# A four-layer residual kernel on one core: x1 goes through memory and back, the step's order changes, and the scores wait by halves

## Chip, cores and metric

The kernel runs on 1 core of one Trainium2 chip. The metric is the device time of one execution in microseconds (us), median of several runs.

## What is computed

`x` is 64 sequences of 64 tokens of 512 float32 numbers. Four layers follow each other, each added to its input:

```python
x0 = x  + x @ W.T + ((x @ A[a].T) @ Bm[a].T) * s[a]      # layer 0: dense, plus an adapter of rank 16 chosen per sequence
x1 = x0 + einsum('bct,bcd->bdt', x0, w1[b])              # layer 1: a 64 x 64 matrix chosen per sequence mixes the tokens
x2 = x1 + attention(x1; Wq, Wk, Wv, Wo, beta)            # layer 2: 16 heads of 32, causal, softmax over 64 tokens
y  = x2 + einsum('bct,bcd->bdt', x2, w3[c])              # layer 3: as layer 1
```

## The kernel before

The 4096 rows of `x` are worked off in 16 pairs of tiles of 128 rows (four sequences a pair). Everything is float32. The dense products are split in two float32r parts (`..._hi`, `..._lo`) and made of three products, hi by hi, hi by lo, lo by hi. The identity of layers 0, 1 and 3 is added to their matrices.

The order on each engine is written out by hand, with semaphores between the engines. After a prologue that turns and splits the five weight matrices and does layers 0 and 1 and the projections of pair 0, there are 16 steps. `in_steps` writes out step 0, loops over steps 1 to 12, and writes out 13 to 15. Step i on TensorE (`step`, L659) is:

1. `values(i)` (L566): the V projection of pair i, 24 matmuls of 512 columns;
2. `layer2_out(i-1)` (L632), 24 matmuls: the output projection of the pair before;
3. `layer0_dense(i+1)`, `adapters_up(i+1)` (L505, L511), 24 and 2 matmuls, into the banks `MIX`;
4. `turn_probs` (L596): transposes of the softmax's rows of pair i, eight for each half g, and between them `layer3(i-1)` and `layer1(i+1)` (both `mix`, L524);
5. `turn_x1(i+1)` (L535): eight transposes of `x1`, since the projections need it with its 512 columns on the partitions (`x1T`); two of VectorE's and ScalarE's copies of PSUM then make `x1T_hi` and `x1T_lo`;
6. `attend()` (L608), probabilities by V for pair i;
7. `key_part` and `query_part` (L556, L561), four of each, for pair i+1: 96 matmuls of 256 columns;
8. `adapters_down(i+2)` (L483), the small product of x with the chosen adapters, and `scores(i+1)` (L581), 64 products of 32 x 64.

The softmax of pair i runs beside 1 to 3. VectorE adds the mask and takes the row maxima (L1029, L1034), GpSimd subtracts them (L1211), ScalarE takes the exponential (L856), VectorE sums and inverts (L1038, L1040). Half 0 is scaled on GpSimd, half 1 on VectorE (L1043). `x` itself is loaded in an arrangement of blocks (`x_blocks`), so that one VectorE transpose of 32 x 32 blocks (`turn_x`, L969) gives `xT` with no TensorE work. GpSimd keeps a copy of `x1` for the residual (`keep_x1`, L1219), which `add_x1` (L1055) adds to layer 2's product. SyncE issues the loads and stores in program order (L395): adapters' rows (`gather_b`, 12 transfers a pair), the store of y, the four block loads of x, and the gathers of w3 and w1.

A matmul of unsplit float32 counts twice in the trace (a `x4` in the program is a `x8` there).

## Time and profile before

| | |
|---|---|
| median of 3 runs (lowest to highest) | 645.58 us (644.78 to 645.97) |
| the profiled execution, its own time | 645.96 us |
| its span from first to last instruction | 644.2 us |
| TensorE busy | 624.6 us, 97% |
| VectorE, ScalarE, GpSimd busy | 389.2 (60%), 211.7 (33%), 140.9 us (22%) |
| granted TensorE clock | full in every one of 40 slices |
| bytes moved | 31.48 MB, mean 49 GB/s |

Busy time says where an engine has work, not what ends last. So this case is read step by step: the time between the same instruction in two steps is what a step costs, and the start of each stage within it tells what each piece holds TensorE for. The duration of a single matmul is longer than its share, since matmuls overlap. The distance from one start to the next is what counts.

### The profile page before, as it was taken

Reading aid. Unit: us, or ns where it says so; the run is one execution under the profiler, and the core shown is the slowest. Engines: PE = TensorE matmul, PEld = TensorE weight load, DVE = VectorE, ACT = ScalarE, POOL = GpSimd, SP = SyncE. Lnnn points to the kernel's source line nnn. Section 1 sums busy time; section 2 is a strip of 40 time slices with the busy share of each in tenths; the row PEclk is TensorE's granted clock in tenths of the full one; section 3 lists DMA queues with packets and bytes.
Section 4 is the critical chain, followed back from the end, with each engine's and each line's share of the span. In section 5 each row is a group of like instructions: output and inputs, shape, how many; then the busy total and the mean of one; then the engine's idle time right before and its main releaser. Section 6 shows DMA issues by size and latency. Waiting matters only on the chain.

```text
span 644.2 us, 19674 instructions
## 1 busy us (share of the span) xinstructions
PE 624.6 (97%) x7814; PEld 524.6 (81%) x7814; DVE 389.2 (60%) x546; ACT 211.7 (33%) x404; POOL 140.9 (22%) x118
## 2 busy tenths in 40 slices
PE   5999999999999999999999999999999999999998
PEld 5787977879888787988879797887988878798885
DVE  3557675656567565666656557565656755556464
ACT  4534333332233232233322223332223323222322
POOL 2005041220403113040310404022040311304031
PEclk9999999999999999999999999999999999999999
DMA  8530102102030110203011020210203011010101
GB/s 266 161 102 20 48 6 61 40 20 73 4 90 8 57 41 13 81 4 90 8 52 46 5 87 5 65 33 22 72 3 90 8 57 42 16 49 2 39 1 66
DMA packets 41110, 31.48 MB, mean 49 GB/s; under 512 B 15546, under 2 KB 30906, under 8 KB 41082
## 3 DMA queue, kind: packets, MB, share of 16 engines
q1 hardware_dynamic: 37130, 25.06, 13.4%
q10 hardware_dynamic: 3952, 6.03, 2.8%
q8 instruction: 19, 0.31, 0.2%
q14 instruction: 9, 0.07, 0.0%
HBM read 22.15 MB, written 8.91 MB: 48 GB/s over the span
## 4 chain that ended last, share of the span: by engine, by line
PE 91%; DVE 4%; DMA 1%; issue 1%; ACT 1%; POOL 0%; ACTq 0%; DVEq 0%
PE banks L547 10%; PE banks L552 9%; PE banks L548 9%; PE banks L599 5%; PE banks L524 5%; PE banks L573 5%; PE banks L641 5%; PE banks L648 5%; PE banks L642 5%; PE banks L575 4%; PE banks L500 4%; PE banks L577 4%; PE banks L498 4%; PE banks L502 4%; PE banks L591 4%; PE banks L615 3%
## 5 line engine op out<-in xcount | busy, mean ns | idle before, releaser
L1211 POOL TENSOR_TENSOR probs<-probs,row_max 128x1024 f32<-128x1024 f32 x32 | 60.9, 1905 | 320.9 <-DVE row_max L1034 320.9
L547 PE MATMUL banks<-x1T_hi,w_hi 128*128 128x256 f32 x512 | 130.6, 287 | 0.2 <-DVE beta L1172 0.2
L548 PE MATMUL banks<-x1T_hi,w_lo 128*128 128x256 f32 x512 | 128.2, 283 | 0.0
L547 PEld LDWEIGHTS banks<-x1T_hi,w_hi 128*128 128x128 f32 x512 | 97.9, 191 | 1.8 <-DVE beta L1172 0.4
L548 PEld LDWEIGHTS banks<-x1T_hi,w_lo 128*128 128x128 f32 x512 | 98.0, 191 | 0.0
L552 PE MATMUL banks<-x1T_lo,w_hi 128*128 128x256 f32 x512 | 82.3, 283 | 0.5 <-issue 0.5
L552 PEld LDWEIGHTS banks<-x1T_lo,w_hi 128*128 128x128 f32 x512 | 70.6, 192 | 0.6 <-issue 0.6
L1020 DVE TENSOR_TENSOR qkT<-banks,beta 128x512 f32<-128x512 f32 x32 | 22.0, 690 | 58.2 <-PE banks L552 58.2
L956 DVE COPY x<-banks 128x512 f32<-128x512 f32 x16 | 11.0, 690 | 72.6 <-PE banks L516 72.6
L1038 DVE TENSOR_REDUCE row_sum<-probs 128x16 f32<-128x1024 f32 x32 | 39.0, 1220 | 25.7 <-ACT probs L856 25.7
L573 PE MATMUL banks<-w_hi,x1T_hi 128*128 128x512 f32 x128 | 51.6, 403 | 1.4 <-issue 0.2
L786 ACT ACTIVATE x<-banks 128x512 f32<-128x512 f32 x16 | 9.6, 597 | 129.3 <-PE banks L516 129.2
L599 PEld LDWEIGHTS banks<-ident,probs 128*128 128x128 f32 x256 | 29.1, 140 | 26.7 <-issue 24.6
L641 PE MATMUL banks<-w_hi,attnT_hi 128*128 128x512 f32 x128 | 50.7, 396 | 0.0
L498 PE MATMUL banks<-w_hi,xT_hi 128*128 128x512 f32 x128 | 50.6, 395 | 0.0
L642 PE MATMUL banks<-w_lo,attnT_hi 128*128 128x512 f32 x128 | 50.5, 395 | 0.0
L500 PE MATMUL banks<-w_lo,xT_hi 128*128 128x512 f32 x128 | 50.0, 391 | 0.0
L575 PE MATMUL banks<-w_lo,x1T_hi 128*128 128x512 f32 x128 | 50.0, 391 | 0.0
L577 PE MATMUL banks<-w_hi,x1T_lo 128*128 128x512 f32 x128 | 50.0, 391 | 0.0
L502 PE MATMUL banks<-w_hi,xT_lo 128*128 128x512 f32 x128 | 49.9, 390 | 0.0
L1029 DVE TENSOR_TENSOR probs<-banks,mask 128x512 f32<-128x512 f32 x64 | 41.1, 684 | 2.5 <-PE banks L591 2.0
L856 ACT ACTIVATE probs<-probs 128x1024 f32<-128x1024 f32 x32 | 34.0, 1061 | 24.5 <-POOL probs L1211 24.5
(130 smaller groups left out, 1067.8 us busy)
## 6 DMA issues: line engine op xcount, KB each, us to landing
x_in<-in_x_dram SPq DMA_DIRECT2D x60, 128.0 KB, 2.4
out_dram<-x_y SPq DMA_DIRECT2D x15, 512.0 KB, 2.8
b_sel<-b_parts SPq DMA_DIRECT2D x180, 32.0 KB, 1.7
w_in<-in_L_cond_weights_dram SPq DMA_DIRECT2D x128, 16.0 KB
probsT<-in_L_cond_W_dram ACTq DMA_DIRECT2D x1, 1024.0 KB, 8.6
probs<-in_L_cond_Wk_dram ACTq DMA_DIRECT2D x1, 1024.0 KB, 7.3
qkT<-in_L_cond_Wq_dram ACTq DMA_DIRECT2D x1, 1024.0 KB, 7.6
probsT<-in_L_cond_Wv_dram ACTq DMA_DIRECT2D x1, 1024.0 KB, 5.1
```

What stands on the lines that cost most here:

```text
L498: nc.tensor.matmul(bank[MIX[t]][:], xT_hi[:, c, tok(t)], w_hi[:, W0, c, :], start=(c == 0), stop=False)
L500: nc.tensor.matmul(bank[MIX[t]][:], xT_hi[:, c, tok(t)], w_lo[:, W0, c, :], start=False, stop=False)
L502: nc.tensor.matmul(bank[MIX[t]][:], xT_lo[:, c, tok(t)], w_hi[:, W0, c, :], start=False, stop=False)
L547: nc.tensor.matmul(out_ap, w_hi[:, w, c, cols], x1T_hi[:, c, :], start=(c == 0), stop=False)
L548: nc.tensor.matmul(out_ap, w_lo[:, w, c, cols], x1T_hi[:, c, :], start=False, stop=False)
L552: last = nc.tensor.matmul(out_ap, w_hi[:, w, c, cols], x1T_lo[:, c, :], start=False, stop=(c == NC - 1))
L573: nc.tensor.matmul(bank[OUT[t]][:], x1T_hi[:, c, tok(t)], w_hi[:, WV, c, :], start=(c == 0), stop=False)
L575: nc.tensor.matmul(bank[OUT[t]][:], x1T_hi[:, c, tok(t)], w_lo[:, WV, c, :], start=False, stop=False)
L577: last = nc.tensor.matmul(bank[OUT[t]][:], x1T_lo[:, c, tok(t)], w_hi[:, WV, c, :], start=False, stop=(c == NC - 1))
L599: last = nc.tensor.transpose(bank[SC[2 * g + n]][:, c * P:(c + 1) * P], probs[:, g, at * P:(at + 1) * P], ident[:])
L641: nc.tensor.matmul(at[:], attnT_hi[:, c, tok(t)], w_hi[:, WO, c, :], start=(c == 0), stop=False)
L642: nc.tensor.matmul(at[:], attnT_hi[:, c, tok(t)], w_lo[:, WO, c, :], start=False, stop=False)
```

## The change

- `x1` of pair i+1 is stored by SyncE to a buffer in memory (`x1_rows`), and loaded again twice: as four transfers in the arrangement of blocks (`x1_in`), which VectorE turns (`turn_x1`, one 128 x 1024 instruction) into `x1T` in SBUF, and as rows (`x1_res`) for the residual. ScalarE and VectorE make `x1T_hi` and `x1T_lo` from that in one instruction each. The eight transposes of `x1` on TensorE are gone for pairs 1 to 15, and so is GpSimd's `keep_x1`. Pair 0 keeps its transposes.
- A step on TensorE begins with `layer0(i+1)` with its adapters. Then come three quarters of the first tile of `values(i)`, its last quarter, `layer1(i+1)`, and the second tile of `values(i)`. Only then comes `layer2_out(i-1)`. `layer3(i-1)` stands behind all the transposes of the probabilities. `adapters_down(i+2)` stands ahead of `attend`.
- Banks: the queries go to banks 0 and 2 (2 is also the first key bank), adapters down to bank 4, y always to `MIX`. So the third query part waits for ScalarE's copy of the first half of the keys. Two groups of weights in the prologue use other banks.
- `scores` waits for keys and queries by halves: the first 32 products for the first half of each, the others for the second.
- The copies of the turned probabilities are three on ScalarE and one on VectorE instead of two each. ScalarE does both exponentials ahead of its copies of V. VectorE turns the next x (`turn_x`) ahead of `add_x1`.
- In the prologue the load of W is issued ahead of that of Bm.

The core of the diff:

```diff
-X1T, Q = SC[0:2], SC[2:4]
+X1T, Q = SC[0:2], (OUT[0], MIX[0])
-DOWN = OUT[1]
+DOWN = SC[0]
+    x1_rows = nc.dram_tensor("x1_rows", [PAIRS, TILES, P, D], F32, kind="Internal").ap()
+    x1_blocks = x1_rows.rearrange("i t (h j) (g n) -> i g j (t h) n", j=SQ, g=JG)
...
@@ SyncE, step @@
+                    at = pair_indices(idx0_row, ADAPTERS, i + 2)
+                    sp.wait_ge(x0_mm, TILES * (i + 2))
+                    gather_b(at, range(2))
+                if after(i, 1):
+                    store_x1(i + 1)
+                if after(i, 2):
+                    gather_b(at, range(2, 3))
+                if after(i, 1):
+                    load_x1_blocks(i + 1)
+                if after(i, 2):
+                    gather_b(at, range(3, 4))
+                load_x1_rows(i)
...
@@ TensorE, scores @@
-                pe.wait_ge(k_copied_act, i + 1)
-                pe.wait_ge(k_copied_dve, i + 1)
-                pe.wait_ge(q_scaled, TILES * (i + 1))
-                for mm in range(NC // 2):
+                for mm, k_copied in enumerate((k_copied_act, k_copied_dve)):
+                    pe.wait_ge(k_copied, i + 1)
+                    pe.wait_ge(q_scaled, 2 * i + mm + 1)
...
@@ TensorE, prologue @@
             for m in range(NC):
+                if m == 2:
+                    pe.wait_ge(k_copied_act, 1)
                 query_part(m)
...
@@ ScalarE, step @@
-                for g in range(HG):
-                    copy_v(i, g)
-                    exp(i, g)
+                exp(i, 0)
                 if nxt:
                     x0_copy(i + 1)
+                exp(i, 1)
+                copy_v(i, 0)
+                if nxt:
+                    x1_copy(i + 1)
+                copy_v(i, 1)
...
@@ VectorE @@
+            def turn_x1(i):
+                dve.wait_ge(x1_in_loaded, 16 * JG * i)
+                nc.vector.transpose(x1T[:].rearrange("p c (b j) -> p b c j", j=SQ),
+                                    x1_in[:].rearrange("p b (e c) -> p b c e", c=NC)).then_inc(x1_turned, 1)
```

TensorE, middle of the looped step, before: `x_both` is x1, L524 is layer 3 and then layer 1, L615 is `attend`.

```order
L516 MATMUL banks<-b_sel,xa_parts 128x512
L599 MATMUL banks<-ident,probs 128x128 [waits probs_done0,x2_added,w3_ready]
L599 MATMUL banks<-ident,probs 128x128 x7
L524 MATMUL banks<-x_y,w_own 64x512 x4
...
L524 MATMUL banks<-x,w_own 64x512 x4
L599 MATMUL banks<-ident,probs 128x128 x7
L537 MATMUL banks<-ident,x_both 128x128 [waits x1_copied_act,pT_copied_dve,pT_copied_act]
L537 MATMUL banks<-ident,x_both 128x128 x3
L537 MATMUL banks<-ident,x_both 128x128 [waits x1_copied_dve]
L537 MATMUL banks<-ident,x_both 128x128 x2
L537 MATMUL banks<-ident,x_both 128x128 [waits pT_copied_act,pT_copied_dve,y_copied_dve,y_copied_act]
L615 MATMUL banks<-probsT,v 32x64 x64
```

The same place now (L630 the probabilities' transposes, L560 layer 3, L528 adapters down, L646 `attend`, L581 the keys):

```order
L630 MATMUL banks<-ident,probs 128x128 [waits probs_done0]
L630 MATMUL banks<-ident,probs 128x128 x7
L630 MATMUL banks<-ident,probs 128x128 [waits probs_done1]
L630 MATMUL banks<-ident,probs 128x128 x6
L630 MATMUL banks<-ident,probs 128x128 [waits x1_copied_act,x1_copied_dve,x2_added,w3_ready]
L560 MATMUL banks<-x_y,w_own 64x512 x4
L636 REGISTER_ALU
L723 REGISTER_ALU [waits pT_copied_dve,pT_copied_act]
L528 MATMUL banks<-xT,a_sel 32x128 [waits x_turned,a_ready,v_copied]
L528 MATMUL banks<-xT,a_sel 32x128 x7
L646 MATMUL banks<-probsT,v 32x64 x64
```

Behind layer 3 TensorE now waits for all copies of the turned probabilities before it has anything to do, and layer 1 has left this place.

VectorE in the looped step now, around the new transpose (L1009 turns x, L1055 turns x1, L1104 is `add_x1`, L1000 the lo part):

```order
L1092 TENSOR_TENSOR probs<-probs,row_inv 128x1024 [waits inv_done]
L1007 REGISTER_ALU
L1009 STREAM_TRANSPOSE xT<-x_in 128x8x4x32 [waits xa_mm,x_loaded]
L1102 REGISTER_ALU
L1103 ISA [waits x1_res_loaded]
L1104 TENSOR_TENSOR x_y<-banks,x_res 128x512 [waits x2_mm]
L1103 REGISTER_ALU [waits x1_res_loaded]
L1104 TENSOR_TENSOR x_y<-banks,x_res 128x512 [waits x2_mm]
L1054 REGISTER_ALU
L1055 STREAM_TRANSPOSE x1T<-x_in 128x8x4x32 [waits x1_in_loaded]
L1107 ISA
L996 COPY probsT<-banks 128x512 [waits pT_mm]
```

The transpose of x1 stands behind the second `add_x1` and ahead of the copy of the probabilities, for which TensorE waits.

The end of the looped step on TensorE, before:

```order
L493 MATMUL banks<-xT,a_sel 32x128 [waits x_turned,a_ready,attn_split]
L493 MATMUL banks<-xT,a_sel 32x128 x7
L591 MATMUL banks<-qkT 64x64 [waits q_scaled,k_copied_dve,k_copied_act]
L591 MATMUL banks<-qkT 64x64 x63
```

and now:

```order
L616 REGISTER_ALU [waits k_copied_act]
L622 MATMUL banks<-qkT 64x64 [waits q_scaled]
L622 MATMUL banks<-qkT 64x64 x31
L616 REGISTER_ALU [waits k_copied_dve]
L622 MATMUL banks<-qkT 64x64 [waits q_scaled]
L622 MATMUL banks<-qkT 64x64 x31
```

The adapters' product no longer stands between the last query part and the scores.

## Rows read from the trace of the kernel before

**Rows 1.** The page, part 1: engine, busy us, share, instructions

```profile
PE 624.6 (97%) x7814; PEld 524.6 (81%) x7814; DVE 389.2 (60%) x546; ACT 211.7 (33%) x404; POOL 140.9 (22%) x118
```

**Rows 2.** The page, part 4: the chain of waits, by engine

```profile
PE 91%; DVE 4%; DMA 1%; issue 1%; ACT 1%; POOL 0%; ACTq 0%; DVEq 0%
```

**Rows 3.** Timeline, step 5 on TensorE: start, duration, engine, line, operation, count, idle before

```profile
234.60 1.58 PE L591 MATMUL banks<-qkT 32*64 32x64 f32 x128 [0.30 <-DVE qkT L1020]
236.31 0.49 PE L573 MATMUL banks<-w_hi,x1T_hi 128*128 128x512 f32 x1
...
253.39 1.04 PE L599 MATMUL banks<-ident,probs 128*128 128x128 f32 x8
254.36 1.09 PE L524 MATMUL banks<-x_y,w_own 64*64 64x512 f32 x8
...
257.52 1.30 PE L537 MATMUL banks<-ident,x_both 128*128 128x128 f32 x8
...
258.76 1.48 PE L615 MATMUL banks<-probsT,v 64*32 64x64 f32 x128
...
260.17 0.38 PE L547 MATMUL banks<-x1T_hi,w_hi 128*128 128x256 f32 x1
...
271.87 0.65 PE L493 MATMUL banks<-xT,a_sel 128*32 128x128 f32 x16
272.81 0.49 PE L591 MATMUL banks<-qkT 32*64 32x64 f32 x33 [0.30 <-DVE qkT L1020]
```

**Rows 4.** Timeline, the same step on VectorE

```profile
244.36 1.22 DVE L1038 TENSOR_REDUCE row_sum<-probs 128x16 f32<-128x1024 f32 x1 [0.94 <-ACT probs L856]
...
245.90 1.23 DVE L1043 TENSOR_TENSOR probs<-probs,row_inv 128x1024 f32<-128x1024 f32 x1
...
257.67 0.69 DVE L956 COPY probsT<-banks 128x512 f32<-128x512 f32 x1
...
262.11 2.09 DVE L969 STREAM_TRANSPOSE xT<-x_in 128x1024 f32<-128x1024 f32 x1
```

**Rows 5.** The page, part 6: DMA issues, KB each, median us to landing

```profile
x_in<-in_x_dram SPq DMA_DIRECT2D x60, 128.0 KB, 2.4
out_dram<-x_y SPq DMA_DIRECT2D x15, 512.0 KB, 2.8
```

**Rows 6.** Timeline, the same step on SyncE's queue

```profile
253.74 5.74 SPq L343 DMA_DIRECT2D b_sel<-b_parts  x12
```

**Rows 7.** Timeline, start of the prologue: two loads, and the first turned weights

```profile
1.25 0.51 ACTq L792 DMA_DIRECT2D x<-in_L_cond_Bm_dram  x1
1.80 0.60 ACTq L789 DMA_DIRECT2D probsT<-in_L_cond_W_dram  x1
...
11.26 3.69 PE L429 MATMUL banks<-ident,probsT 128*128 128x128 f32 x16 [2.44 <-DVE probsT L1142]
```

**Rows 8.** Timeline, end of the prologue: third query part, copy of keys, scores, values

```profile
41.59 0.28 PE L547 MATMUL banks<-x1T_hi,w_hi 128*128 128x256 f32 x1
...
45.28 0.58 ACT L786 ACTIVATE qkT<-banks 128x512 f32<-128x512 f32 x1
...
46.52 1.65 PE L591 MATMUL banks<-qkT 32*64 32x64 f32 x128 [0.41 <-DVE qkT L1020]
48.11 0.50 PE L573 MATMUL banks<-w_hi,x1T_hi 128*128 128x512 f32 x1
```

**Rows 9.** Timeline, step 0: its first key product, and the first product of step 1

```profile
65.99 0.38 PE L547 MATMUL banks<-x1T_hi,w_hi 128*128 128x256 f32 x1
...
83.17 0.50 PE L573 MATMUL banks<-w_hi,x1T_hi 128*128 128x512 f32 x1
```

**Rows 10.** Timeline, last step: values, output projection of pair 14, second exponential

```profile
617.79 0.50 PE L573 MATMUL banks<-w_hi,x1T_hi 128*128 128x512 f32 x1
...
623.38 0.40 PE L641 MATMUL banks<-w_hi,attnT_hi 128*128 128x512 f32 x1
...
624.91 1.06 ACT L856 ACTIVATE probs<-probs 128x1024 f32<-128x1024 f32 x1 [0.73 <-POOL probs L1211]
```

More of the change, by code:

```diff
@@ L292, in after @@
             return not isinstance(i, int) or 0 <= i + n < PAIRS
-        def out_banks(i):
-            return OUT if after(i, 1) else MIX
         def last_attn(ap, t, r):
@@ L335, in gather, with gather_b @@
                                  table[bass.ds(at[n], 1), :, :].rearrange("a c e -> (a c) e")).then_inc(arrived, 16)
-            def gather_b(at):
-                for n in range(PSEQ):
+            def gather_b(at, which=range(PSEQ)):
+                for n in which:
                     t, b = divmod(n, SEQT)
@@ L350, in load_x, with one_pair, store_x1, load_x1_blocks @@
                         .then_inc(x_loaded, 16)
+            def one_pair(ap, i, pattern):
+                return ap[i] if isinstance(i, int) else ap[bass.ds(i, 1)].rearrange(pattern)
+            def store_x1(i):
+                sp.wait_ge(x1_copied_act, i + 1)
+                sp.wait_ge(x1_copied_dve, i + 1)
+                sp.dma_start(one_pair(x1_rows, i, "a t p d -> (a t) p d").rearrange("t p d -> p t d"), x1[:])\
+                    .then_inc(x1_stored, 16)
+            def load_x1_blocks(i):
+                sp.wait_ge(x1_stored, 16 * (i + 1))
+                for g in range(JG):
+                    sp.dma_start(x1_in[g * SQ:(g + 1) * SQ], x1_blocks[i, g] if isinstance(i, int)
+                                 else x1_blocks[bass.ds(i, 1), g].rearrange("a j b n -> (a j) b n"))\
+                        .then_inc(x1_in_loaded, 16)
+            def load_x1_rows(i):
+                if after(i, -1):
+                    sp.wait_ge(x2_added, TILES * i)
+                else:
+                    sp.wait_ge(x1_stored, 16)
+                sp.dma_start(x1_res[:], one_pair(x1_rows, i, "a t p d -> (a t) p d").rearrange("t p d -> p t d"))\
+                    .then_inc(x1_res_loaded, 16)
             def store_y(i):
@@ L695, in step @@
                     pe.wait_ge(y_copied_dve, i)
-                else:
-                    pe.wait_ge(v_copied, TILES)
-                pT_copied(i, HG)
-                turn_x1(i + 1, 1, range(NC - 1, NC))
-                attend()
-                pe.wait_ge(x1_hi_done, TILES * (i + 2))
                 for m in range(NC):
@@ L1064, in step @@
                     mask_and_max(i, g)
-                for g in range(HG):
-                    sums(i, g)
+                if nxt:
+                    x0_copy(i + 1)
+                sums(i, 0)
+                if nxt:
+                    x1_copy(i + 1)
+                sums(i, 1)
+                if nxt2:
+                    turn_x(i + 2)
                 if prev:
```

251 lines of the change are left out of this document (122 added, 129 removed).

## The prediction

> **What bounds the kernel now.** I read the busy shares first, then the chain of waits, then one middle step on the timeline. TensorE is busy 97% of the span, VectorE 60% [rows 1], and 91% of the chain that ended last is TensorE's [rows 2]. So the time is what TensorE's queue takes plus the holes in it. A step lasts from one start of the scores to the next, 272.81 - 234.60 = 38.21 us [rows 3]. Within it the reader should see two things. The eight transposes of x1 hold TensorE from 257.52 to 258.76, 1.24 us. And from the last query product to the first score, 271.87 to 272.81, 0.94 us pass, although the adapters' product in between is busy for only 0.65: the releaser is VectorE's scaling of q [rows 3].
>
> **A middle step, part by part.**
>
> - The x1 transposes go: **-1.24** us, with a short wait inside them.
> - Scores by halves. Before, 0.94 us pass behind the last query product, then the scores hold TensorE for 1.6 (1.58 busy; 1.71 to the next product in step 5). Now the first half starts at once and runs beside the scaling, and the second half starts 0.94 behind the queries: 0.94 + 0.8 instead of 0.94 + 1.6, **-0.80**.
> - The adapters' product lay beside that scaling and cost nothing. Now it stands in the open ahead of `attend`: at most its 0.65, and less by what the last matmul overlaps with the next product; I take **+0.40**.
> - Layer 1 now cuts the values in two, one more change of kind each way. Such a change costs about 0.1: the first value product starts 1.71 behind the first score, though the scores are busy for 1.58 [rows 3]. **+0.10**.
> - The queue of VectorE. With T = 0 at the end of the scores, TensorE does layer 0 (5.6), adapters up (0.45), values in two parts with layer 1 (2.0 + 0.7 + 1.0 + 2.7, plus the change) and `layer2_out` (5.5): it ends at 18.1. Layer 2's second half is then added on VectorE (0.2 to notice, 0.65, a little under a copy's 0.69 since two in a row overlap), then x1 is turned (2.09, as the same instruction on x takes [rows 4]), then the copy of probabilities (0.69 [rows 4]) follows: at 18.1 + 0.2 + 0.65 + 2.09 + 0.69 + 0.1 = 21.8. TensorE meanwhile does two lots of eight transposes (0.97 each, 253.39 to 254.36 [rows 3]), layer 3 (1.02) and one change: 18.1 + 3.1 = 21.2. It waits **+0.55**. The ends of this are 0 (if the copy's wait is hidden) and 0.8.
>
> Sum -0.99; I take -1.0 per step. Steps 1 to 13 are alike: **-13.0**. Step 14 has no adapters to do in either kernel: -1.24 - 0.80 + 0.10 + 0.55, **-1.4**.
>
> **Is x1 back in time?** This is what the step rests on. VectorE copies x0 at 6.2, sums half 0 and copies x1 at 10.0 to 10.7. Then come the sum of half 1, its inverse and its scaling (244.36 to 245.90, then 1.23 [rows 4]), and x is turned until 15.5. SyncE issues six of the adapters' transfers from 6.1 at 5.74/12 = 0.48 each [rows 6], done at 9.0, so the store of x1 goes at 10.7. A store of 512 KB lands after 2.8, a block load of 128 KB after 2.4 [rows 5]. Three more adapter transfers pass while the store is under way. So the loads are issued from 13.5, the last at 14.9, and land at 17.3. VectorE is free for the transpose at 18.95. The margin is 1.6 us. The hi part on ScalarE ends at 22.2 (about 1.06, as the exponential of the same size [rows 10]) and `attend` at 23.7, so the keys don't wait for it. Layer 1 doesn't wait either: x0 is copied at 6.9, layer 1 starts at 8.7.
>
> GpSimd's copy of x1 goes, and nothing waited for it. The 24 MB more in memory traffic lie beside a queue that is mostly empty. The residual's load has a whole step.
>
> **Where cover is missing.**
>
> - *Prologue.* W's load is issued 0.55 earlier [rows 7], and the 256 KB of Bm no longer share the way. Between 0.55 and 1.5 us come off; I take **-1.0**. But the third query part, at 41.59, must now wait for the first keys to be copied, and ScalarE does that at 45.28 to 45.86, behind four selections of adapters [rows 8]. Restart at 45.95, two query parts 2.88, adapters down 0.4, then xa_low on ScalarE and its sum on VectorE, for which the scores now wait (0.85), scores 1.6: 51.7 instead of 48.11 [rows 8]. **+3.6**.
> - *Step 0* has no `layer2_out` and no layer 3 to cover the trip through memory. TensorE is through with values and transposes at T + 14.5; the blocks land at 17.3, the transpose ends at 19.6, the copy of probabilities at 20.3. Then adapters down 0.4, attend 1.41 (258.76 to 260.17 [rows 3]), the projections with Wo's transposes 14.6 (17.18 less 0.94 and 1.6), and 0.94 + 0.8: 38.5. Before, step 0 took 83.17 - 48.11 = 35.06, of which 17.18 from the first key product on [rows 8, 9]. **+3.5**.
> - *Last step.* The copy of the first half of V now comes behind both exponentials. The second ends at 624.91 + 1.06, and the copy takes 0.6, so `layer2_out(14)` starts 8.9 behind the start of the values instead of 5.59 [rows 10]. Nothing else waits there: **+3.3**.
> - *The clock.* The two holes, 4.4 us in the prologue and 5.9 in step 0, are longer than any hole in the trace once TensorE runs at pace. In the prologue, behind a hole of 2.44 and slow work ahead of it, 16 transposes take 3.69 us, 0.22 each [rows 7], where a later eight take 0.97 [rows 3]. That slow stretch lasts to about 16.4, five us, and loses some 2.6 there. So each hole costs between 0 and 2.6; the nearer row, for the longer one, is the slow stretch. I take **+2.0** for step 0 and 0 for the prologue.
>
> Sum: -13.0 - 1.4 - 1.0 + 3.6 + 3.5 + 3.3 + 2.0 = **-3.0**. The durations are those of the profiled execution (645.96, span 644.2), which stands 0.38 above the median. I set the change against the median: 645.58 - 3.0 = **642.6 us**.
>
> The Trainium skill ("TensorE: Matmul & The Clock Gate", What's actually happening) says that TensorE falls back to 1.2 GHz when it has been idle and gets 2.4 GHz only after a stretch of work. By it both holes may be paid, up to 2.6 more than my sum. The profile's slices call the granted clock full even where the 16 transposes took 0.22 each, so they don't settle it here.
>
> **Rivals.**
>
> 1. *The trip through memory is late* (the slower side). Nothing in the trace reads from memory what was just written within microseconds and is waited for. If the blocks land behind T + 18.95, VectorE's transpose, the copy behind it and TensorE wait one for one, in 14 steps, and step 0 pays the whole excess over 17.3. From there on each us costs 15. A landing at 19.3, 2 us later than I have it, gives 14 x 0.35 + 2 = +7 on my sum: **649.5 us**, slower. It decides from +0.2 us past the margin. For it: the store can't be issued before 10.7, behind six transfers, and the four loads wait for its landing. Against: with the slowest landings in the traffic, one us more on each leg, it is still within the margin or just at it.
> 2. *No waits behind the turn, no clock loss.* If VectorE's copy is no later than TensorE's transposes and the holes don't lower the clock, 14 x 0.55 + 2.0 come off: **632.9 us**. For it: the slack is only half a us. Against: the order puts transpose and copy one behind the other.
> 3. *The steps give back less than the ends take.* If switching between kinds and the wait each cost 0.2 more, 14 x 0.25 = 3.5 come back, and if the prologue's hole costs its 2.6: **648.7 us**; with one of the two, about 646, no change.
> 4. *The transposes were the right place.* The work moved is 1.24 us of TensorE for 2.09 of VectorE and five transfers. Should the projections be held up by x1T instead (its hi part ends at 22.2, 1.5 ahead of the keys), the step is as long as before and the ends' +11.4 remain: above 655 us. Nothing in the sums above points there.
>
> The Trainium skill ("VectorE: DVE Perf Modes", Rules for kernel authors) gives 128 x 128 transposes to TensorE when PSUM may hold the result, and 32 x 32 ones to VectorE. By it the change goes the wrong way, and case 4 would hold; the trace shows TensorE as the bound and a turned x made of 32 x 32 blocks in 2.09 us [rows 4], which speaks against the rule here.
>
> **How the numbers follow.** Forecast 0.50 (639 to 646), case 1 0.17, case 2 0.15, case 3 0.15, case 4 0.03. A measurement here can tell about 0.2%, 1.3 us. Faster by more: 0.43 of the forecast's half and case 2, 0.58. Within: 0.06 of the forecast and 0.08 of case 3, 0.14. Slower: 0.01, cases 1 and 4, and 0.07 of case 3, 0.28. The range reaches down most of the way to case 2 and up to case 1's price: **636 to 649.5**.
>
> **What would show it.** Right: no x1 transposes from step 1 on; middle steps of 37.2 us; TensorE waiting about 0.5 for VectorE's copy of probabilities ahead of adapters down; scores split with a hole of about 0.15 in the middle; about 4.4 us of waiting at the third query part, 5.9 in step 0, 3.3 ahead of `layer2_out(14)`. Wrong: VectorE's transpose of x1 waiting for a DMA in the middle steps (case 1), middle steps under 36.8 (case 2), or key products of 0.24 us start to start behind a hole in the prologue as well (case 3).

## The result, and the profile after

| | before | after |
|---|---|---|
| median (lowest to highest), runs on the same chip | 645.48 us (644.78 to 645.97) | 657.19 us (656.03 to 658.17) |
| span of the profiled execution | 644.2 us | 654.3 us |
| TensorE busy | 624.6 us, 97% | 614.9 us, 94% |
| mean granted TensorE clock | 1.000 | 0.987 |
| bytes moved | 31.48 MB | 56.12 MB |

The change makes the kernel slower: the ratio is 1.018 (95% interval 1.016 to 1.019), small but clear of the noise, where a gain of 0.5% was forecast. TensorE is busy for 9.7 us less and the span is 10.1 us longer, so some 20 us more go into holes. Part of the busy time is now spent at the lower clock, so the work itself shrank by more than 9.7 us. The page of the kernel after, part 1, answers to [rows 1]; under it the row of part 2 with the granted clock in 40 slices of 16.4 us:

```profile
PE 614.9 (94%) x7694; PEld 516.9 (79%) x7694; DVE 399.6 (61%) x530; ACT 215.0 (33%) x405; POOL 109.0 (17%) x101
...
PEclk9989699999999999999999999999999999999999
```

The reader should see the 6 in the fifth slice: that is step 0. The 8 in the third slice is the prologue. Before, every slice was a 9. The waits of TensorE say where the holes are (us in total, times, longest):

```profile
PE banks L528 <- DVE probsT L996: 17.5, 13, 6.7
PE banks L485 <- DMA x_y<-in_x_dram: 4.2, 1, 4.2
PE banks L581 <- ACT qkT L821: 4.1, 1, 4.1
PE banks L672 <- ACT v L821: 2.9, 1, 2.9
PE banks L581 <- issue: 1.6, 1, 1.6
```

The second is the first load of x, at the very start, and as old as a wait of 1.7 us for turned weights that is left out here. The first is the wait ahead of `adapters_down` for VectorE's copy of the turned probabilities, 6.7 in step 0 and 0.9 in the looped steps. The third is the third query part of the prologue, the fourth `layer2_out(14)` in the last step. The last, 1.6 us in which TensorE waited for nothing that the profile shows, is new.

By stages, each from the first product behind a `scores` to the next such product:

| | before | after | difference | forecast |
|---|---|---|---|---|
| start to the end of `scores(0)` | 48.11 | 52.55 | +4.44 | +2.6 |
| step 0 | 35.06 | 42.92 | +7.86 | +5.5 |
| steps 1 to 14 | 534.62 | 529.38 | -5.24 | -14.4 |
| last step, to the end | 26.4 | 29.45 | +3.05 | +3.3 |
| sum | 644.2 | 654.3 | +10.1 | -3.0 |

**The prologue.** TensorE's timeline, third query part and what follows, answers to [rows 8]:

```profile
45.12 0.39 PE L581 MATMUL banks<-x1T_hi,w_hi 128*128 128x256 f32 x1 [4.13 <-ACT qkT L821]
...
48.01 0.41 PE L581 MATMUL banks<-x1T_hi,w_hi 128*128 128x256 f32 x1
48.22 0.41 PE L582 MATMUL banks<-x1T_hi,w_lo 128*128 128x256 f32 x1
...
49.67 0.65 PE L528 MATMUL banks<-xT,a_sel 128*32 128x128 f32 x16
51.02 1.59 PE L622 MATMUL banks<-qkT 32*64 32x64 f32 x128 [0.71 <-DVE xa_sum L1018]
52.55 0.50 PE L533 MATMUL banks<-w_hi,xT_hi 128*128 128x512 f32 x1
```

The wait of 4.13 us is the forecast one. Behind it the products of 256 columns start 0.21 apart instead of 0.12: the two query parts take 49.67 - 45.12 = 4.55 us where 2.88 were counted. So this hole costs 1.67 more than itself.

**Step 0.** The same engine and then VectorE and SyncE's queue. T is here and below the start of the step's first product, 52.55:

```profile
66.59 1.09 PE L630 MATMUL banks<-ident,probs 128*128 128x128 f32 x8 [0.21 <-DVE probs L1092]
74.41 1.08 PE L528 MATMUL banks<-xT,a_sel 128*32 128x128 f32 x16 [6.72 <-DVE probsT L996]
75.42 2.05 PE L646 MATMUL banks<-probsT,v 64*32 64x64 f32 x128
```

```profile
66.45 2.02 DVE L1009 STREAM_TRANSPOSE xT<-x_in 128x1024 f32<-128x1024 f32 x1
71.75 1.99 DVE L1055 STREAM_TRANSPOSE x1T<-x_in 128x1024 f32<-128x1024 f32 x1 [3.27 <-DMA x_in<-x_rows]
73.66 0.65 DVE L996 COPY probsT<-banks 128x512 f32<-128x512 f32 x1
```

```profile
63.94 0.41 SPq L361 DMA_DIRECT2D x_rows<-x  x1
...
66.82 2.02 SPq L367 DMA_DIRECT2D x_in<-x_rows  x4
```

The store is issued at T + 11.4, the loads from T + 14.3, and the blocks are there at T + 19.2. VectorE's copy stands behind the turn of these blocks, and TensorE behind the copy, so both wait for them. How the clock answers is in the windows (us, TensorE busy, granted clock, DMA share, GB/s):

```profile
67.00:69.00 2.00, 0.68 (x7) 1.00 0.53 145
69.00:71.00 2.00, 0.00 (x0) 0.59 0.83 161
71.00:73.00 2.00, 0.00 (x0) 0.50 0.63 195
...
81.00:83.00 2.00, 2.00 (x11) 0.50 0.04 8
83.00:85.00 2.00, 2.00 (x19) 1.00 0.12 25
```

TensorE stops at about 67.7; in the window from 69 the granted clock is 0.59, then 0.50, the lower of its two levels (1.2 of 2.4 GHz), and it is full again from 83, 8.6 us behind the restart at 74.41.

**A middle step** takes 37.75 us instead of 38.20 [rows 3]. TensorE and VectorE in step 7 (T = 323.95), around the adapters:

```profile
344.14 1.09 PE L560 MATMUL banks<-x_y,w_own 64*64 64x512 f32 x8
346.13 0.64 PE L528 MATMUL banks<-xT,a_sel 128*32 128x128 f32 x16 [0.89 <-DVE probsT L996]
346.70 1.48 PE L646 MATMUL banks<-probsT,v 64*32 64x64 f32 x128
```

```profile
342.50 0.69 DVE L1104 TENSOR_TENSOR x_y<-banks,x_res 128x512 f32<-128x512 f32 x1 [2.10 <-PE banks L679]
343.11 2.10 DVE L1055 STREAM_TRANSPOSE x1T<-x_in 128x1024 f32<-128x1024 f32 x1
345.12 0.67 DVE L996 COPY probsT<-banks 128x512 f32<-128x512 f32 x1
```

VectorE's transpose waits for no transfer here; it starts as soon as `add_x1` is done. Layer 3 holds TensorE for 1.02 us, until 344.14 + 1.02 = 345.16, so 0.97 us pass to 346.13.

**The last step.** `layer2_out(14)` waits for the copy of V behind both exponentials:

```profile
633.56 0.50 PE L672 MATMUL banks<-w_hi,attnT_hi 128*128 128x512 f32 x1 [2.93 <-ACT v L821]
```

### The profile page after: what moved, and what is told of

It is laid out like the page before. It is cut to its first block, busy times and chain, and to the rows that moved or that the text cites. A ratio compares the mean times of both kernels' runs of the same rounds, so it can differ in the third digit from the quotient of the medians.

```text
span 654.3 us, 19780 instructions
## 1 busy us (share of the span) xinstructions
PE 614.9 (94%) x7694; PEld 516.9 (79%) x7694; DVE 399.6 (61%) x530; ACT 215.0 (33%) x405; POOL 109.0 (17%) x101
## 2 busy tenths in 40 slices
DMA packets 66134, 56.12 MB, mean 86 GB/s; under 512 B 17018, under 2 KB 47738, under 8 KB 66106
## 4 chain that ended last, share of the span: by engine, by line
PE 87%; issue 5%; DVE 5%; DMA 1%; ACT 1%; POOL 0%; ACTq 0%; SPq 0%; DVEq 0%
PE banks L581 10%; PE banks L582 9%; PE banks L586 9%; PE banks L533 5%; PE banks L672 5%; PE banks L679 5%; PE banks L673 5%; PE banks L604 5%; PE banks L535 4%; PE banks L537 4%; PE banks L622 4%; PE banks L608 4%; PE banks L606 4%; PE banks L646 3%; PE banks L560 3%
## 5 line engine op out<-in xcount | busy, mean ns | idle before, releaser
L581 PE MATMUL banks<-x1T_hi,w_hi 128*128 128x256 f32 x512 | 133.1, 291 | 5.7 <-ACT qkT L821 4.1
L582 PE MATMUL banks<-x1T_hi,w_lo 128*128 128x256 f32 x512 | 130.6, 287 | 0.4 <-issue 0.4
L581 PEld LDWEIGHTS banks<-x1T_hi,w_hi 128*128 128x128 f32 x512 | 99.9, 195 | 7.7 <-ACT qkT L821 4.3
L582 PEld LDWEIGHTS banks<-x1T_hi,w_lo 128*128 128x128 f32 x512 | 99.9, 195 | 0.7 <-issue 0.7
L533 PE MATMUL banks<-w_hi,xT_hi 128*128 128x512 f32 x128 | 52.2, 408 | 1.4 <-issue 0.2
L996 DVE COPY x<-banks 128x512 f32<-128x512 f32 x32 | 22.1, 691 | 47.0 <-PE banks L560 27.4
L1104 DVE TENSOR_TENSOR x_y<-banks,x_res 128x512 f32<-128x512 f32 x32 | 22.1, 692 | 42.7 <-PE banks L679 42.7
L1244 POOL TENSOR_TENSOR w_own<-w_in,own 128x128 f32<-128x128 f32 x32 | 14.0, 455 | 191.9 <-PE banks L560 165.3
L821 ACT ACTIVATE probsT<-banks 128x512 f32<-128x512 f32 x48 | 26.8, 596 | 46.1 <-PE banks L630 46.1
```

Source lines behind the costliest of these rows:

```text
L533: nc.tensor.matmul(bank[MIX[t]][:], xT_hi[:, c, tok(t)], w_hi[:, W0, c, :], start=(c == 0), stop=False)
L581: nc.tensor.matmul(out_ap, w_hi[:, w, c, cols], x1T_hi[:, c, :], start=(c == 0), stop=False)
L582: nc.tensor.matmul(out_ap, w_lo[:, w, c, cols], x1T_hi[:, c, :], start=False, stop=False)
```

## The experiments

The theory after the result: the steps' gain is real but VectorE's queue eats most of it, and the ends cost four separate waits, two of which bring the lower clock with them. The rival: the trip through memory costs in every step, by its latency or by its traffic. The medians of before beside the runs were 646.2 to 646.3. A trace is one execution of a version, and the whole times of five of them (scores whole, all on TensorE, later trip, step 0 on TensorE, idle transposes) are medians of two runs each. Dots in the diffs stand for lines that are not shown.

**ScalarE makes all four copies.**

```diff
...
-            for g, n in ((0, 0), (0, 1), (1, 1)):
+            for g, n in ((0, 0), (0, 1), (1, 0), (1, 1)):
...
-                copy_pT(i)
```

> The changed kernel, but ScalarE makes all four copies of the turned probabilities, and VectorE none. Theory (in each middle step TensorE waits 0.97 us in front of adapters_down because VectorE turns x1 for 2.10 us ahead of its copy): the wait falls to 0.3 to 0.4 us, a middle step takes 37.1 to 37.2 us instead of 37.75, steps 1 to 14 some 8 us less, the whole about 649. In step 0 ScalarE's copies are no longer behind the trip through memory; there the wait moves to the first key product, which needs the turned x1, and the gain is at most 1.5 us. Rival (ScalarE, with four copies of 0.6 us in a row behind the last transposes, takes as long as VectorE did): the hole stays at 0.9 and the time at 657. Second rival (the hi part of the turned x1, which ScalarE makes after them, comes too late for the keys): a new wait in front of the first key product.

Measured: 645.04 us, 0.998 of before (0.997 to 1.000); a middle step takes 36.87. TensorE in step 7 of this version:

```profile
337.98 1.09 PE L560 MATMUL banks<-x_y,w_own 64*64 64x512 f32 x8
339.08 0.64 PE L528 MATMUL banks<-xT,a_sel 128*32 128x128 f32 x16
```

The wait is gone altogether, not down to 0.3: -0.88 per step, 12 us in all. Both rivals fall in the middle steps. In step 0 the second one holds, as expected: the first key product waits 0.79 us for the hi part of x1, and the step takes only 1.0 us less. This one queue decides between a slower kernel and an even one.

**The scores whole again.**

```diff
+                pe.wait_ge(k_copied_act, i + 1)
+                pe.wait_ge(k_copied_dve, i + 1)
+                pe.wait_ge(q_scaled, 2 * i + 2)
-                for mm, k_copied in enumerate((k_copied_act, k_copied_dve)):
-                    pe.wait_ge(k_copied, i + 1)
-                    pe.wait_ge(q_scaled, 2 * i + mm + 1)
+                for mm in range(2):
```

> The changed kernel with the scores whole again: they start when both halves of q are scaled and both halves of the keys copied. Theory (each step saves by the split the 0.8 us that the first half takes beside VectorE's scaling): the scores start 0.8 us later after the last query product in each of 15 steps, a middle step takes 38.5 to 38.6 us instead of 37.75, and the whole some 12 us more than the changed kernel, about 669. Rival (the split is worth little, since what saves time in the step is only that the x1 transposes left TensorE): a middle step under 38.0, the whole under 661.

Measured: 668.53 us, a middle step 38.49. The split is worth 0.74 us per step; -0.80 was forecast. Without it the change would have no gain in the steps at all.

**x1 turned by TensorE in every step.**

```diff
                 pT_copied(i)
+                for t in range(TILES):
+                    turn_first_x1(t, SC[2:4])
...
-                if nxt:
-                    turn_x1(i + 1)
```

> The changed kernel, but TensorE turns x1 in every step (eight transposes behind its wait for the turned probabilities); the block loads still run and nothing reads them, and VectorE's turn of x1 is gone. Theory (the trip saves TensorE 1.24 us per step and costs it 0.88 of waiting for VectorE's queue, so it brings only some 0.4): a middle step takes 37.75 - 0.9 + 1.24 = 38.1 us, and step 0 about 38.6 as with x1 turned by TensorE there alone. Whole: 13 x 0.35 more and 4 less than the changed kernel, about 658. Rival (the transfers of the trip slow something else in each step, which then goes on): above 38.4 per step. Second rival (the wait for VectorE's copy does not come from the turn ahead of it): the wait stays at 0.9 and a middle step takes 39.0.

Measured: a middle step takes 37.95 us, only 0.20 more than with the trip through memory. There is no wait behind layer 3, and the eight transposes hold TensorE for 1.16 us:

```profile
349.54 1.23 PE L573 MATMUL banks<-ident,x 128*128 128x128 f32 x8
350.70 0.64 PE L528 MATMUL banks<-xT,a_sel 128*32 128x128 f32 x16
```

So -1.24 from the transposes and +0.9 for VectorE's queue nearly cancel: as it stands the trip is worth 0.2 us a step. The whole, 661.92 us (659.9 and 663.9), is above the 658 expected: two waits for nothing the profile shows last 4.8 us together, the larger in step 1, which took 43.1 us, the other in step 0, which took 41.8 and not 38.6. Behind each the clock was at or near 0.5 for a few us, and the trace is that of the slower of the two runs. The other experiments have them too, and below they are taken up by themselves.

**The trip through memory a little later.**

```diff
-                    gather_b(at, range(2))
+                    gather_b(at)
                 if after(i, 1):
                     store_x1(i + 1)
-                if after(i, 2):
-                    gather_b(at, range(2, 3))
...
-                if after(i, 2):
-                    gather_b(at, range(3, 4))
```

> The changed kernel, but SyncE issues all twelve of the adapters' transfers ahead of the store of x1, so x1's trip through memory starts later, by 3 to 6 issues of 0.48 us: the store at about T + 12 instead of T + 11.0 and the loads in one go behind its landing, at T + 15 instead of 14.0. Theory (in the middle steps the trip has over a microsecond of slack before VectorE turns x1 at T + 19.1): nothing changes in the middle steps, 37.75, and step 0 takes about 1 us more, so the whole 1 to 2 us more, about 658. Rival (the trip through memory is what TensorE waits for in front of adapters_down in every step): each step takes up to 1 us more, the whole about 670.

Measured: a middle step takes 38.17 us, +0.42; the whole came out at 660.0 and 666.0 in two runs, with a wide interval. Queue and VectorE in one step (T = 286.31):

```profile
298.68 0.42 SPq L361 DMA_DIRECT2D x_rows<-x  x1
301.54 1.90 SPq L367 DMA_DIRECT2D x_in<-x_rows  x4
```

```profile
304.87 0.69 DVE L1100 TENSOR_TENSOR x_y<-banks,x_res 128x512 f32<-128x512 f32 x1 [2.10 <-PE banks L675]
305.89 2.09 DVE L1051 STREAM_TRANSPOSE x1T<-x_in 128x1024 f32<-128x1024 f32 x1 [0.33 <-DMA x_in<-x_rows]
307.86 0.69 DVE L992 COPY probsT<-banks 128x512 f32<-128x512 f32 x1
```

The loads start at T + 15.2 instead of T + 14.0, 1.2 us later, and VectorE's transpose now waits for them, 0.33 to 0.4. My expectation was wrong here, and this shows the slack of the trip as it stands: 1.2 - 0.4 = 0.8 us, half of the 1.6 that the prediction had. The trace of the changed kernel has it directly: in the looped step that starts at 210.71 the last block lands at 229.13, 0.74 us before VectorE turns to it at 229.87. So it is just enough, and the latency rival falls for the middle steps. With the twelve adapters' transfers all ahead of the store it comes true. In step 0 the expectation, 1 us more, failed too: the hole grew from 6.7 to 7.4 us, yet the step took 41.2 instead of 42.7, since the full clock was back about 4.5 us behind the restart and not 8.6.

**The prologue: keys copied first.**

```diff
             take_matrix(WV)
+            copy_k(0)
             x_hi(1)
...
             select_a(1)
-            copy_k(0)
```

> The changed kernel, but in the prologue ScalarE copies the first keys ahead of splitting x and selecting adapters for pair 1. Theory (the third query part waits only because this copy stands late in ScalarE's queue, and what follows the wait runs at half clock): the wait of 4.3 us in front of the third query part falls under 0.3, the third and fourth query parts take about 2.9 us again instead of 4.55, and the first product behind scores(0) starts at about 48 instead of 52.55, so about 4.5 us less than the changed kernel, some 652.5. Rival (the prologue is bound by the adapters of pair 1, which now come later and hold up the scores): the wait moves behind the queries, and under 2 us come back.

Measured: `scores(0)` start at 45.64 instead of 51.02, the wait of 4.1 us is not in the list, and the clock is full from 40 to 50: 5.4 us come back, 1.7 of them the clock's. The whole is 651.9 us (eight runs, from 648.8 to 655.3, a wider spread than any version of before). The spread goes with the clock: the mean granted clock is 0.995 in the three runs under 650 us and 0.987 to 0.992 in the five others. The trace is that of the fastest run. In it step 0 too is 2.1 us shorter than in the changed kernel, although its hole is as long (6.56 us), because the full clock is back about 3 us behind the restart.

**Step 0: x1 of pair 1 turned by TensorE.**

```diff
+                if not prev:
+                    for t in range(TILES):
+                        turn_first_x1(t, SC[2:4])
...
-                if nxt:
+                if nxt and prev:
                     turn_x1(i + 1)
```

> The changed kernel, but x1 of pair 1 is turned by TensorE in step 0 (eight transposes behind the wait for the turned probabilities), and does not come back in blocks from memory; all later steps as changed. Theory (step 0 has too little work to cover the trip through memory, and the hole costs its own length and then the half clock behind it): the hole of 6.72 us shrinks to about 1, the clock stays at 1.0, step 0 takes 36 us instead of 42.9, the whole some 650. Rival (step 0 is long because of its own extra work, the transposes of Wo and the split of it): step 0 stays over 40 us.

Measured: 653.97 us, step 0 from scores to scores 38.6 where it was 42.67, not the 36 expected. A hole of 3.4 us stays. ScalarE, and TensorE behind it (T = 53.62):

```profile
69.56 1.06 ACT L824 ACTIVATE xT_hi<-xT 128x1024 fp32r<-128x1024 f32 x1 [2.37 <-DVE xT L1014]
70.52 1.55 ACT L824 ACTIVATE probsT<-banks 128x512 f32<-128x512 f32 x3
```

```profile
72.13 1.98 PE L573 MATMUL banks<-ident,x 128*128 128x128 f32 x8 [3.40 <-ACT probsT L824]
```

There was a second wait under the first. ScalarE's copies of the probabilities stand behind its split of the next x, that behind VectorE's `turn_x`, and that behind the softmax. In a middle step `layer2_out` covers this; in step 0 nothing does. It held TensorE until T + 18.5 with no trip at all. And the clock is down for it as well (the eight transposes take 1.98 us).

**Step 0: TensorE kept busy while it waits.** This one does 52 transposes more, whose result nothing uses.

```diff
+                if not prev:
+                    for n in range(52):
+                        nc.tensor.transpose(bank[MIX[1]][:, n % NC * P:(n % NC + 1) * P], ident[:], ident[:])
                 pT_copied(i)
```

> The changed kernel with 52 more transposes of the identity on TensorE in step 0, in front of its wait for the turned probabilities; nothing reads what they write. They take about 0.12 us each, 6.3 us in all, so they fill most of the hole of 6.72 us and leave the end of the wait where it is. Theory (the hole costs its length and, behind it, a half clock until about 83 us): the hole is still paid in full but the stretch from its end to the start of scores(1) takes some 18.2 us instead of 21.06, so 2.9 us less than the changed kernel, about 654.3. Rival (that stretch is long for another reason, the splitting of Wo on ScalarE and VectorE): no difference, 657, with the granted clock at 1.0 all the same. The second rival: idle transposes do not hold the clock, which then still reads 0.5 behind them.

TensorE in step 0, and the window of the stretch behind:

```profile
68.09 5.84 PE L721 MATMUL banks<-ident 128*128 128x128 f32 x52
75.53 0.64 PE L528 MATMUL banks<-xT,a_sel 128*32 128x128 f32 x16 [1.60 <-issue]
76.11 1.49 PE L646 MATMUL banks<-probsT,v 64*32 64x64 f32 x128
```

```profile
78.00:80.00 2.00, 2.00 (x19) 1.00 0.17 35
```

The clock holds at 1.00 throughout. From the restart at 75.53 to the first product behind the next scores, at 92.70, 17.2 us pass where it was 21.06. Of these 3.9, 0.4 are a wait that this run does not have, so the lower clock costs about 3.5 us in the changed kernel's trace, over the 2.9 expected. Measured in the same way it costs 1.7 in the trace with the later trip and 1.2 in that with the prologue changed, whose holes are about as long (7.4 and 6.6 us): so the price of the hole is not fixed. The idle transposes buy it back, though the wait itself ends no earlier. The 1.60 us in front of the restart are still the wait for VectorE's copy, which ends at 75.43, though the profile names no releaser. The whole, 660.92, is slower all the same: step 13 takes 40.76 instead of 37.5, and the end 5.5 us more. Waits of 1.60 and 2.19 us for nothing the profile shows stand there, behind each the clock falls to 0.5, and it does so behind the hole ahead of `layer2_out(14)` as well. The inserted work moved the later code. That these waits changed place and length for that reason is likely, not shown.

**Five moves together.** The two of ScalarE above and the last step's (copies of V ahead of the exponentials), and in step 0 `x_hi(2)` behind the copies and x1 turned by TensorE into free banks:

```diff
+                if not prev:
+                    pe.wait_ge(pT_copied_act, 2)
+                    for t in range(TILES):
+                        turn_first_x1(t, (SC[1], MIX[1]))
                 pT_copied(i)
...
+                if not nxt:
+                    copy_v(i, 0)
                 exp(i, 0)
+                if not nxt:
+                    copy_v(i, 1)
```

> Five moves on the changed kernel: the first keys copied ahead of x_hi(1) in the prologue; ScalarE making all four copies of the turned probabilities; in step 0 x1 turned by TensorE, ahead of its wait for the turned probabilities and into two free banks, without the trip; in step 0 x_hi(2) behind those copies in ScalarE's queue; in the last step the copies of V ahead of the exponentials. Theory (the changed kernel loses by these five places of its queues alone): scores(0) starts at 45.6, step 0 takes 34 to 35 us with the clock at 1.0, a middle step 36.9, the last step 3 us less: some 629 us. Rival (in step 0 the hole stays, for a reason other than the trip and x_hi(2), the softmax chain through GpSimd): step 0 at 38, the whole about 633. Second rival (stretches that wait for nothing the profile shows grow with each rearranged program, as in the run with 52 idle transposes): 632 or more with such waits in the list.

Measured: 632.07 us, 0.978 of before (0.976 to 0.979), faster than both kernels. `scores(0)` start at 45.59, a middle step takes 36.87, and from the last scores to the end 28.0 us pass where it was 31.2: each as expected. Step 0 is not, at 39.3: its wait for the copies is gone, but the products of probabilities and values stop in the middle. (The trace is that of the slowest of the four runs, with a mean clock of 0.992 where the others have 0.995 to 0.997, so not every run loses as much there.)

```profile
63.93 1.42 PE L645 MATMUL banks<-probsT,v 64*32 64x64 f32 x121
68.47 0.43 PE L645 MATMUL banks<-probsT,v 64*32 64x64 f32 x7 [3.13 <-issue]
```

```profile
64.00:66.00 2.00, 1.34 (x121) 1.00 0.99 292
66.00:68.00 2.00, 0.00 (x0) 1.00 1.12 204
68.00:70.00 2.00, 1.52 (x12) 0.52 0.22 42
```

They stop while the 16 DMA engines are as good as full (share 0.99 and 1.12), with 512 KB of x1's rows and 512 KB of the next x behind each other. The page lists queues of kind instruction among the DMA queues:

```profile
q8 instruction: 19, 0.31, 0.2%
```

(packets, MB, share). The waits of this kind come in the written-out steps and in the first pass of the loop, where code runs for the first time; in passes 2 to 12 there is none over 0.3 us.

The trace holds the start of every single packet, and this says what TensorE waits for. Queue q8 moves 16 KB at a time, in the prologue, in steps 0 and 1 and from step 13 on; once pass 2 is under way it moves nothing until step 13. Here a packet starts at 65.95 and TensorE goes on at 68.47. In all thirteen traces together 20 waits of 0.4 us or more, from step 0 on, have no releaser and no copy that ends just ahead of them. Every one of them ends 2.3 to 2.9 us behind the start of such a packet. The timing says that TensorE waits there for its own code, though no run changed the delivery of code alone. Most packets bring no wait: those that do fall beside or right behind `attend`, where TensorE runs 128 small products in 1.5 us. The other waits without a releaser, those of 0.7 us and more ahead of adapters down or `attend` in steps 13 and 14, end 0.1 us behind VectorE's copy of the probabilities. They are the wait for that copy.

**x1's rows loaded later.** In the changed kernel, and in the version with the five moves:

```diff
-                load_x1_rows(i)
+                if not after(i, 1):
+                    load_x1_rows(i)
...
                 if after(i, 3):
                     gather_w1(i + 3)
+                if after(i, 1):
+                    load_x1_rows(i)
```

> The changed kernel, but the load of x1's rows for the residual (512 KB) is issued at the end of SyncE's step, behind the loads of the weight rows, and not right ahead of the 512 KB of x. Theory (the stretches of 1 to 3 us in which TensorE waits for nothing the profile shows stand where the program runs code for the first time while a megabyte lands at 170 to 290 GB/s; its instructions are then late, since they come through the same DMA engines): the wait of 1.58 us in step 1 falls under 0.5, step 1 takes 37.8 to 38.2 instead of 39.5, middle steps stay at 37.75, the whole some 1.6 us less than the changed kernel, 655.6. Rival (the wait belongs to the place in the program, not to the transfers): step 1 stays at 39.5. Second rival (the load is then late for the addition of x1): VectorE waits for the rows in every step and the time rises.

> The version with the five moves, and in it the load of x1's rows at the end of SyncE's step. Theory: the wait of 3.13 us in step 0's product of probabilities and values, and the half clock behind it, go (39.3 falls to 34 to 35.5), and step 1 takes about 38 instead of 40.1; middle steps 36.87; the whole 6 to 8 us less than with the five moves alone, 624 to 627. Rival (such waits only move to the next place where a transfer is large): a wait of over a microsecond stays in step 0 or 1, and the whole is 629 or more.

Measured in the changed kernel: step 1 takes 37.99 instead of 39.52, and the wait of 1.58 us (121.36 to 122.94) is gone. A window of TensorE just ahead of it, first in the changed kernel, then in this one:

```profile
118.00:120.00 2.00, 2.00 (x143) 1.00 1.21 228
```

```profile
118.00:120.00 2.00, 1.81 (x136) 1.00 0.08 16
```

The 16 KB packet of code starts at T + 24.8 in the changed kernel and at T + 23.3 here: the megabyte held it up by 1.5 us, the length of the wait. But a middle step takes 37.85, 0.1 more, and the whole is 656.84 (654.5 to 657.4), not told apart from the changed kernel's 657.19. In the trace the last step undoes the gain. It takes 31.0 us instead of 29.45, because the clock falls behind its hole of 2.96 us, which it did not behind the 2.93 of the changed kernel:

```profile
634.00:636.00 2.00, 2.00 (x6) 0.50 0.00 0
```

With the five moves: 630.95 us, 0.977 of before (0.975 to 0.978), some 1 us less than without it, where 6 to 8 were expected. Steps 0 and 1 give back 2.1 and 2.0 us, and the middle steps take 0.1 more each. In step 0 a wait of 2.3 us stays, at half the traffic, and one of 1.2 in step 1 stands where hardly anything is transferred:

```profile
66.00:68.00 2.00, 0.00 (x0) 1.00 0.49 126
...
108.00:110.00 2.00, 1.11 (x49) 1.00 0.04 8
```

**The kernel before, with 512 KB more in a step.** A load of x by rows ahead of that in blocks; nothing reads it.

```diff
+                sp.dma_start(unread[:], x_v[i] if isinstance(i, int)
+                             else x_v[bass.ds(i, 1)].rearrange("a p t d -> (a p) t d")).then_inc(unread_loaded, 16)
                 if after(i, 3):
                     turned_in(i + 3)
```

> The kernel before with one transfer more in each step: 512 KB of x by rows into a tile that nothing reads, issued ahead of the load of x in blocks. Theory (a megabyte in one go, where code runs for the first time, holds up TensorE's instructions): a wait for nothing that the profile shows, of 1 us or more, appears in step 0 or 1, which hardly has one now (0.2 us), and the middle steps stay at 38.20; the whole is 1 to 3 us more, about 648. Rival: no such wait, the time within 0.2% of the kernel before.

Measured: 646.32 us against 646.31, ratio 1.000 (0.999 to 1.001). Step 1 takes 38.97 where it was 38.38, step 0 35.38 where it was 35.04, and a wait of 0.8 us stands in step 0. The packet of code in step 0 starts at the same place, T + 17.4 in both, but takes 1.36 us instead of 0.93, and the wait grew by 0.34. The direction is that of the theory, the size is not, and the rival's time came out. So full DMA engines are one part of these waits only: they delay or stretch the packet. With little traffic TensorE still waited 1.2 us for one. What decides when a packet is asked for, and so how long TensorE waits, was not tried by itself and stays open.

## Why the prediction was wrong, step by step

- *The sign.* The forecast was -3.0, the outcome +10.1 in the span. Of the 13.1 between them, steps 1 to 14 account for 9.2, step 0 for 2.4, the prologue for 1.8, and the last step for -0.2. So the step that failed is the gain of 1.0 us per middle step: 0.45 came, because the wait behind VectorE's queue was 0.97 and not 0.55, the adapters cost 0.57 and not 0.40, and the split scores brought 0.74 and not 0.80.
- *The step, -1.0 forecast, -0.45 measured.* Here the prediction failed, 13 times over. The transposes went, as said. The split of the scores brought 0.74 (0.80). The adapters in the open cost 0.57 (+0.40 taken; the "at most its 0.65" was nearer, since the matmuls behind overlap them hardly at all). The largest miss is **the queue of VectorE, +0.55 taken, 0.97 measured**. Its two ends were nearly right: the copy ends at T + 21.84 where 21.8 stood, which already held 0.1 for TensorE to notice it, and TensorE is through at T + 21.2 as forecast. The prediction's own two ends are 0.6 apart, of which it took 0.55. But from the end of the copy to the adapters' first product 0.34 us pass. In the written-out steps 0 and 13 only 0.10 pass, so the looped steps cost 0.24 more there. The looped wait compares against a computed count, which may be the reason; that was not tried. The stated upper end, 0.8, was too low. What the copy's place behind a 2.1 us instruction costs is read from the experiment that gave this copy to ScalarE: 0.88 per step. I named the queue, and sized it 0.42 too low, nearly as much as a step gained in the end. The four measured terms, -1.24, -0.74, +0.57 and +0.97, add up to -0.44; nothing is left for the +0.10 of layer 1's change of kind.
- *Step 1* has 1.6 us more, a wait for nothing the profile shows, in no term of the sum.
- *Is x1 back in time?* In the middle steps yes, as forecast, but the margin is 0.7 to 0.8, not 1.6: the loads go out 0.5 later than said, and the last lands 2.9 us behind its issue and not 2.4.
- *Step 0, +3.5 and +2.0 for the clock; +7.86 measured.* The mechanism and the place were right. **The trip was mis-sized**: the blocks land at T + 19.2, not 17.3. The loads start 0.8 later, and the last lands 3.2 behind its issue instead of the 2.4 of [rows 5], which was measured for the same arrangement with other data and a quieter queue. That made the restart 1.5 later. Behind it the clock cost about 3.5, over the 2.6 that bounded it; the work there was 1.0 shorter than counted, which hides part of that. Two other traces paid only 1.2 and 1.7 for about as long a hole, so no single figure would have been safe. The second wait, ScalarE's split of x ahead of the copies, I did not see; it alone takes until T + 18.5.
- *The prologue, +2.6; +4.44 measured.* The wait is 4.13 (4.36 forecast). **Its clock was taken at 0 and cost 1.67**, within the bound of 2.6. The sign to look for, key or query products at twice their distance, is there. The rule of the Trainium skill ("TensorE: Matmul & The Clock Gate", What's actually happening), a fall to 1.2 GHz when TensorE has been idle, was the better guide: by it both holes are paid, and the trace agrees, with 1.67 and about 3.5 us. The third hole, 2.93 us in the last step, was not paid in this trace.
- *The last step, +3.3; +3.05 measured.* Right, cause and size, with some luck: the lower clock, for which nothing was put down, stayed away here and came in four other traces.
- *The rivals.* Case 1 has a late trip only in step 0. Case 2 is refuted. Case 3, steps that give back less and a paid prologue's hole, is what happened, with twice the size it was given: 0.25 per step was 0.55, and step 0's clock and trip came on top. Its sum was not clean either, for two costs of 0.2 each make 0.4 a step and not 0.25. Case 4's mechanism did not occur in the changed kernel, since `x1T` is never late for the keys; that the whole, 657.19, lies above its 655 is chance. But its verdict on the transposes nearly holds: turned on TensorE in every step they cost 0.20 per step more, and in step 0 alone they save 4.1. The Trainium skill's rule ("VectorE: DVE Perf Modes", Rules for kernel authors), 128 x 128 transposes to TensorE, comes within 0.20 us a step of being right as long as VectorE's copy stands behind its transpose. Once it does not, VectorE's way is 1.08 us a step better (36.87 against 37.95).

## What to carry to other kernels

Work taken off the bounding engine is worth what is left after the queue that it joins: look at what stands behind it there, and whether the bounding engine waits for that. Here one copy moved to another engine turned +12 us into 0, and five moves with one load issued later, without any change to what is computed, made 657 into 631. Price the ends of the pipeline apart from its middle: steps without a predecessor have none of the cover that the middle has, and on TensorE a hole of 4 to 7 us cost 1.2 to 3.5 more in clock behind it here. Read the mean granted clock of several runs before trusting one trace's price. Where one wait is removed in such a step, ask at once which second one lies under it.

## What the hardware showed that was not expected

- Behind a hole of 4.13 us TensorE ran at the lower clock for about 3.5 us of work, behind one of 6.72 for about 8.6, and behind one of 3.13, in the version with the five moves, for some 6. Behind the 0.97 of the middle steps it never did. The length of the hole does not settle it: behind the 2.9 to 3.0 us ahead of `layer2_out(14)` the clock stayed full in five traces and fell to 0.50 in four, which cost 1.5 us; it fell behind a wait of 1.60 in step 13 of the run with idle transposes, and stayed full behind one of 2.54 in step 1 of the run with x1 turned by TensorE in step 0.
- 52 transposes of 0.11 us each, back to back, kept the full clock through a wait of 7.4 us.
- TensorE can wait up to 3.5 us for its own code, where that runs for the first time. Such waits sum to 0.5 us in the kernel before and to as much as 4.9 in the others (five moves). Each ends 2.3 to 2.9 us behind the start of a 16 KB packet of an instruction queue, and 512 KB of other traffic more delayed one such packet by 1.5 us. The profile gives them no releaser.
- Some versions spread more from run to run (648.8 to 655.3 in one). The spread goes with the mean granted clock, 0.995 to 0.987.
- A store of 512 KB and the loads of the same bytes in blocks, one behind the other, took 71.75 - 63.94 = 7.8 us from the issue of the store to the start of the instruction that waits for the blocks.
